# Gated cross-attention with an int8-style FFN on one core: attention rebuilt as a software pipeline, with operand turns by DMA and one block for both phases

## What is computed

```python
x = x + tanh(g_xattn) * xattn(layernorm(x), ctx)        # causal, softmax over 256 keys
x = x + tanh(g_ffn) * ffn(layernorm(x))
# xattn: q = xn @ Wq.T; k, v = split(ctx @ Wkv.T); softmax(causal(q k^T / sqrt(32))) v @ Wout.T
# ffn:   xq, w1q, w2q, hq are the operands rounded to 127 steps of their rows' maxima
#        gate, up = split(xq @ w1q.T); h = silu(gate) * up; hq @ w2q.T
```

## Time and profile before

| | us |
|---|---|
| median of 3 runs | 884.68 (880.06 to 885.18) |
| the profiled execution, its own time | 884.49 |
| its span in the profile | 882.4 |
| TensorE busy | 782.7 (89%) |
| VectorE busy | 638.7 (72%) |
| GpSimd busy | 518.5 (59%) |
| ScalarE busy | 418.2 (47%) |
| granted TensorE clock, mean | 0.955 of full |
| DMA | 135.98 MB |

### The profile page before, as it was taken

How to read it: one execution, slowest core, us unless ns; L and a number is a source line. 1 busy time by engine, 2 the same in 40 slices (tenths; PEclk the granted TensorE clock), 3 DMA queues, 4 the chain that set the end, 5 groups by cost and what they waited for, 6 DMA issues and landing times. The chain is left out here.

```text
span 882.4 us, 19003 instructions
## 1 busy us (share of the span) xinstructions
PE 782.7 (89%) x6146; PEld 564.8 (64%) x6168; DVE 638.7 (72%) x1997; ACT 418.2 (47%) x664; POOL 518.5 (59%) x671
## 2 busy tenths in 40 slices
PE   2579899998999989989999999897699999999994
PEld 2468787886877877868878778675444444444441
DVE  3575776876866867768678576476389999999992
ACT  5336456466375464563664645414234444444441
POOL 3525466474564663754745637324167888888885
PEclk9788899999999999999999999977899999999998
DMA  5784765775857757768668575406115655565666
GB/s 211 176 195 130 173 164 150 179 191 140 212 150 180 173 161 164 179 147 204 168 164 190 144 179 124 125 2 269 61 23 117 160 151 140 139 139 139 144 140 168
DMA packets 121889, 135.98 MB, mean 154 GB/s; under 512 B 73536, under 2 KB 84288, under 8 KB 121536
## 3 DMA queue, kind: packets, MB, share of 16 engines
q1 hardware_dynamic: 120768, 134.26, 60.0%
q10 hardware_dynamic: 1024, 0.53, 0.2%
HBM read 47.06 MB, written 25.30 MB: 82 GB/s over the span
## 5 line engine op out<-in xcount | busy, mean ns | idle before, releaser
L654 DVE CUSTOM_DVE_ANT_0 junk<-psum,mask 128x128 f32<-128x128 f32 (+1 forms) x512 | 159.4, 354 | 5.0 <-PE psum L843 3.2
L1172 PE MATMUL psum<-w1q,xqb 128*128 128x512 bf16 (+1 forms) x757 | 157.7, 363 | 3.3 <-PEq L255 1.9
L1072 POOL TENSOR_TENSOR up<-gate,up 128x512 f32<-128x512 f32 (+1 forms) x96 | 112.4, 1185 | 46.1 <-ACT gate L1098 38.3
L390 POOL TENSOR_SCALAR_AFFINE_SELECT prob<-prob 128x512 f32<-128x512 f32 x128 | 80.2, 638 | 94.5 <-ACT prob L588 87.0
L1172 PEld LDWEIGHTS psum<-w1q,xqb 128*128 128x128 bf16 x768 | 75.4, 98 | 83.9 <-issue 4.0
L1103 ACT ACTIVATE up<-up,round_bias,hinv 128x1408 f32<-128x1408 f32 x32 | 50.0, 1561 | 128.7 <-DVE hinv L1144 128.7
L588 ACT ACTIVATE prob<-psum 128x768 f32<-128x768 f32 x128 | 101.5, 827 | 18.4 <-PE psum L912 18.0
L910 PE MATMUL psum<-qs,ks 98*128 98x256 f32 x256 | 78.8, 369 | 23.8 <-DMA qs<-nmT 18.6
L1186 PE MATMUL psum<-w2q,hqT 128*128 128x512 bf16 x341 | 81.8, 389 | 7.4 <-DMA hqT<-hq 6.8
L910 PEld LDWEIGHTS psum<-qs,ks 98*128 98x128 f32 x256 | 50.8, 199 | 44.6 <-DMA qs<-nmT 25.9
L843 PE MATMUL psum<-ks,qs 96*128 96x256 f32 x256 | 76.1, 344 | 0.0
(11 more groups left out here) (126 smaller groups left out, 1904.2 us busy)
## 6 DMA issues: line engine op xcount, KB each, us to landing
ks<-k_hi SPq DMA_DIRECT2D x128, 128.0 KB, 2.7
qs<-q_hi SPq DMA_DIRECT2D x128, 128.0 KB, 2.4
xln<-x_dram SPq DMA_DIRECT2D x16, 512.0 KB, 5.0
ks<-k_lo SPq DMA_DIRECT2D x64, 128.0 KB, 2.5
qs<-q_lo SPq DMA_DIRECT2D x64, 128.0 KB, 2.9
x<-x_dram SPq DMA_DIRECT2D x16, 512.0 KB, 3.9
x_scratch<-x SPq DMA_DIRECT2D x16, 512.0 KB, 5.1
x1b<-x_scratch SPq DMA_DIRECT2D x32, 256.0 KB, 3.5
```

What stands on the lines that cost most here:

```text
L390: pool.affine_select(out=blk, in_=blk, compare_op=ALU.is_ge, fill=0.0, base=0, pattern=[[0, 4], [1, P]], channel_multiplier=-1).then_inc(s ...
L654: dve.tensor_tensor_reduce(junk[:, n % 2, 0:w], psum[:, h % 4, cols], m, 1.0, LOWEST, ALU.add, ALU.max, mx[:, par, t, h:h + 1]).then_inc(s ...
L1072: pool.tensor_tensor(up[:, t % 3, o], gate[:, t % 3, o], up[:, t % 3, o], ALU.mult).then_inc(f["prod_done"], 1)
L1172: last = pe.matmul(psum[:, n, 0:w], xqb[:, t % 4, k, :], w1q[:, k, half * I + o:half * I + o + w], start=(k == 0), stop=(k == KH - 1))
```

## The change

- All runs in one block. Slots b go from -2 to 16; tile 0 of the FFN stands between slots 15 and 16 on every engine, tiles 1 to 35 behind slot 16.
- In slot b, PE does the output of T = b-1, pass two and `weigh` of A = b, pass one of N = b+1, and transposes, keys, queries, values of F = b+2. Passes one and two alternate, two heads and one pair at a time. Pass one has banks 0 and 1, one head each, pass two has banks 2 and 3 for every pair. Reciprocals and both broadcasts of A lie at the end of the same slot.
- `WORK`, and with it the banks 6 and 7, is new.
- Weights are stored as rows and read back in slot 14 with two transposing DMAs; rounded x is stored as rows and loaded tile by tile with a transposing DMA. The scales go to DRAM in slot 13 and come back as broadcast loads. PE's and DVE's work on these is gone.
- `stand_alone`, which only incremented an unused semaphore, is gone. The FFN's operations are the same.

The diff, cut to its core:

```diff
-        WORK = [("K", 0, 1), ("K", 1, 1), ("Q", 0, 1), ("BC", 0, -1), ("BC", 1, -1), ("Q", 1, 1), ("V", 0, 1),
-                ("XT", 0, -2), ("O", 0, -1), ("O", 1, -1), ("V", 1, 1), ("XT", 1, -2), ("T", 0, 2), ("T", 1, 2),
-                ("W", 0, 1), ("W", 1, 1)]
+        WORK = [("O", 0, -1), ("O", 1, -1), ("T", 0, 2), ("T", 1, 2), ("K", 0, 2), ("K", 1, 2), ("Q", 0, 2),
+                ("BC", 0, 0), ("Q", 1, 2), ("BC", 1, 0), ("V", 0, 2), ("V", 1, 2)]
+        def run(eng, slot, tile):
+            for b in range(-2, B):
+                slot(b)
+            tile(0)
+            slot(B)
+            for t in range(1, NT + 4):
+                tile(t)
...
@@ sync
+                def load_x(tile):
+                    sp.wait_ge(s["xq_stored"], DMA * (tile // ST + 1))
+                    sp.dma_start_transpose(xqb[:, tile % 4], xq_scratch[tile]).then_inc(f[f"x_loaded{tile % 4}"], DMA)
+                def slot(b):
+                    A, F, T = b, b + 2, b - 1
+                    if b == B - 2:
+                        sp.wait_ge(s["q_moved"], DMA * MOVES * B)
+                        sp.wait_ge(s["k_moved"], DMA * MOVES * B)
+                        sp.wait_ge(s["v_done"], 2 * B)
+                        sp.wait_ge(s["w_stored"], DMA * PIECES)
+                        sp.wait_ge(s["steps_stored"], DMA)
...
+                        sp.dma_start_transpose(w1q[:], w1_scratch).then_inc(f["w1_loaded"], DMA)
+                        sp.dma_start(s1[:], rows[:, 0:2 * I].broadcast_to((P, 2 * I))).then_inc(f["steps_loaded"], DMA)
+                        sp.dma_start(s2[:], rows[:, 2 * I:NW * P].broadcast_to((P, H))).then_inc(f["steps_loaded"], DMA)
+                        sp.dma_start_transpose(w2q[:], w2_scratch).then_inc(f["w2_loaded"], DMA)
...
+                    if present(F + 1):
+                        sp.wait_ge(s["t_done"], 2 * (F + 1))
+                        sp.dma_start(xln[:], x_tok[F + 1]).then_inc(s["x_loaded"], DMA)
...
+                    if b == PIECES - 2:
+                        sp.wait_ge(s["gate_step"], 1)
+                        sp.dma_start(step_scratch.rearrange("n p -> p n"), w_scale[:],
+                                     allow_slow_non_contiguous=True).then_inc(s["steps_stored"], DMA)
+                    if present(T):
+                        sp.wait_ge(s["x1_done"], 2 * T + 2)
+                        sp.dma_start(x1_bat[T], x1[:]).then_inc(s["x1_stored"], DMA)
+                    if present(F):
+                        wait_for(sp, s["st_done"], PAIRS * (A + 1))
+                        spread_heads(k_hi, k_lo, ks, (0, 1, 0), s["k_moved"], s["k_hi"], s["k_lo"], F)
+                    if present(A):
+                        wait_for(sp, s["xn2_done"], 2 * (T + 1))
+                        wait_for(sp, s["x1_stored"], DMA * (T + 1))
+                        sp.dma_start(x1[:], x_tok[A]).then_inc(s["xres_loaded"], DMA)
+                    if present(F):
+                        spread_heads(q_hi, q_lo, qs, (0, 0, 1), s["q_moved"], s["q_hi"], s["q_lo"], F)
+                    if present(T):
+                        sp.wait_ge(s["xq_done"], 2 * T + 2)
+                        sp.dma_start(xq_bat[T], xq[:]).then_inc(s["xq_stored"], DMA)
...
@@ gpsimd, the order of one slot (low_o, select: batch A; quantise, rsqrt2: T; the others: F)
+                    split_context(); rsqrt1(); weights()
+                    if b == -2: tables()
+                    select(0); select(1); low_t(0); select(2); select(3); low_t(1); select(4)
+                    rsqrt2(); select(5); low_k(0); select(6); select(7); low_k(1)
+                    low_o(0); quantise(0); low_o(1); quantise(1)
@@ scalar, the order of one slot
+                    if b > -2: weights()
+                    exps(0); norm1(0); exps(1); norm1(1); exps(2); high_t(0); exps(3); copy_u(0)
+                    exps(4); high_t(1); exps(5); norm2(0); copy_u(1)
+                    if b == -2: high_weights("wq", wq_hi, wq_raw); weights()
+                    exps(6); high_k(0); exps(7); norm2(1); copy_u(2); high_k(1); copy_u(3)
+                    high_q(0); maxima_rows(); high_o(0); high_q(1); high_o(1); copy_v(0); copy_v(1)
@@ vector, the order of one slot
+                    measure_x()
+                    residual(0); measure(0); maxima(0); maxima(1); residual(1); maxima(2); maxima(3)
+                    measure(1)
+                    for h in range(4, NHEAD):
+                        maxima(h)
+                    negate(); reciprocals(); split_q(0); step(0); normalise(0); split_q(1)
+                    normalise(1); step(1); weigh_rows(b + 3)
+                    if b == PIECES - 2:
+                        dve.tensor_scalar(w_scale[:, W1T:NW], w_scale[:, W1T:NW], gates[:, 1:2], None,
+                                          ALU.mult).then_inc(s["gate_step"], 1)
@@ tensor
+                    def scores(h): ...
+                            wait_for(pe, s["max_done"], 2 * (NHEAD * N + h - 1))
+                    def score_pair(pair): ...
+                        wait_for(pe, s["exp_done"], PAIRS * A + pair)
+                    output(0, 0); output(0, 1); score_pair(0); output(1, 0); score_pair(1); output(1, 1)
+                    scores(0); scores(1); score_pair(2); transposed(0); scores(2); scores(3)
+                    score_pair(3); weigh(0); scores(4); scores(5); score_pair(4); transposed(1)
+                    scores(6); scores(7); score_pair(5); weigh(1); scores(8); scores(9)
+                    score_pair(6); keys(0); scores(10); scores(11); score_pair(7); weigh(2)
+                    scores(12); scores(13); keys(1); queries(0); scores(14); scores(15); weigh(3)
+                    queries(1); maxima_rows(); queries(2); broadcast(0); queries(3); broadcast(1)
+                    values(0); values(1)
```

More of the change, by code:

```diff
@@ L337, in _ @@
+                run(sp, slot, tile)
+                for p in range(2):
+                    sp.wait_ge(f[f"stored{p}"], DMA * NT // 2)
             @block.gpsimd
@@ L1106, in slot, with low_weights @@
                     silu(2)
[L1108 removed]
+                run(act, slot, tile)
             @block.vector
             def _(dve):
[L1112 to L1114 removed]
+                dve.memset(round_bias[:], ROUND).then_inc(s["table"], 1)
+                def low_weights(n, hi, lo, raw):
+                    dve.wait_ge(s["high"], n + 1)
+                    dve.tensor_tensor(lo[:], raw, hi[:].bitcast(F32), ALU.subtract).then_inc(s["split"], 1)
```

1373 lines of the change are left out of this document (624 added, 749 removed).

## The result

The change made the kernel slower: 959.05 us (median of 4, 947.73 to 960.87) against 884.93 us for the kernel before (4 runs, 880.06 to 886.74). The ratio is 1.0824, with a 95% interval of 1.0743 to 1.0904. The forecast was 916 us with a range of 880 to 945: the direction was right, the size was not, and the result lies outside the range. The profiled execution after took 960.04 us for a span of 958.3.

What follows compares the result with a forecast made beforehand. Attention was taken as bound by the in-order chain through TensorE with short waits, the FFN by TensorE. 109 + 12 x 37.6 + 50 + 52 + 252.3 gave a 914.3 span, plus 2.1: 916 us, range 880 to 945.

Steps and rivals of the forecast that it cites:

- The walk: Steady attention slot, followed operation by operation: 29 us of TensorE work plus 7.6 of waits, 36.6 in all.
- the 1.0 that the sum has for the clock: Steady slot: allowance for the granted clock falling behind two gaps of 2.2 us, taking a slot from 36.6 to 37.6.
- the 3.0 of its upper bound: Steady slot: most that clock falls were allowed to add, the upper bound of a slot being 39.6 us against 36.6.
- The rival in which the clock stays at 2.4 GHz: Steady slots: no clock fall, 12 slots of 36.6, time 904 us; chance 0.18.
- that of two falls in every slot: Steady slots: clock falls twice a slot, uncovered, 12 slots of 39.6, time 940 us; chance 0.08.
- The rival that ends faster: Steady slots: the norm2 wait is covered, a slot takes 34 or less, time 866 us; chance 0.13.
- with 2.5 for issue and drain of the steps: Slot 13: store of the weight scales taken at 2.5 us from a span of 2.5 to 16, slot about 50.
- a chance of 0.11 together with slow transposes: Rival: steps' store at 16 us, or transposes out of DRAM at half rate (+22), time 930 to 938; chance 0.11.
- The queue on SP: Slot 14: weight transposes, steps' broadcast and x take 28 us ahead of the x1 store; first FFN matmul at +52.
- the 45 without the queue: Drain, slot 14's first scores to the first FFN matmul: 45 us if SP's queue did not delay the x1 load.
- the queue hides: Drain rival: transposes run at the plain DMA rate, so SP's queue costs nothing, time 909 us; chance 0.08.
- 16 heads at 0.62: Start, behind the first scores: VectorE's maxima for 16 heads take 9.9 us, part of reaching batch 1's scores at 74.

Runs made afterwards that it cites:

- the first experiment: The changed kernel with slot 13's store of the weight scales issued behind the last batch's k and q moves instead of ahead: 941.87 us, ratio 1.067.
- third, the bank change: The changed kernel with the second half of the queries in bank 7 instead of 6 and values(0) ahead of broadcast(1): 952.66 us, ratio 1.0766.
- fourth: The changed kernel with norm2(0) on ScalarE behind exps(6) and high_k(0) instead of behind exps(5): 918.33 us, ratio 1.0383.
- fifth experiment: The changed kernel with useless matmuls put into TensorE's three waits in slots 1 to 13: 955.54 us, ratio 1.0808.
- the last kernels: The changed kernel with TensorE-turned scales, norm2(0) later, x1 load before weight transposes, low_t first: 885.81 us; also second queries in bank 7, high_q(1) before high_o(0): 875.87.

## Why the prediction was right or wrong

**Right: the steady slot.** The walk gave 36.6 at full clock, and the slots at full clock average 36.9. No row or run shows the 1.0 that the sum has for the clock, or the 3.0 of its upper bound; in their place the slots show 1.15 (the mean of 38.06 less 36.9) and at most 3.3 (40.2). Each wait that was named is there with its releaser, and the period, which was called the most dangerous term, missed by 0.46, or 5.5 us over 12 slots (0.9 a slot in the first experiment's trace of the same slots). The rival in which the clock stays at 2.4 GHz is refuted by the 1.2 GHz stretches in the trace, and so is that of two falls in every slot: five of the twelve slots have no such stretch, and only one (40.2) is beyond its 39.6.

**Right: the place of the cheap remedy.** The rival that ends faster named the `norm2(0)` wait and a slot of 34 or less. Its mechanism is real: with `norm2(0)` behind `exps(6)` the shortest slots take 34.0 and the mean is 35.3. The price was higher than the 2.25 us of the wait, for the clock goes with it.

**Wrong: slot 13, +18.4.** The step that failed is "with 2.5 for issue and drain of the steps". It is the largest miss: without it the span would have been 939.9. The wait for `gate_step` and the order on SP were right (51.8 measured with long pieces against 50), but of the two ends named, 2.5 and 16 us, the lower one was taken without a reason, and the store took 17.1 to land. The upper end came from a row that was misread. The 128 KB that landed in 4.8 us are 512 pieces of 256 bytes, not 1024; by the piece that makes 31 us for 3328, where 1024 would make 15.6. The trace has 5.1 ns a piece, so neither the bytes nor that row's pieces gave the size, and 16 was near by luck. The store also slowed its neighbours (804 ns a packet against 109) and left a backlog in which the last q move took 10.2 us to land, which no bound contained. The prediction gave this a chance of 0.11 together with slow transposes, and priced the two as one. The Trainium skill (DMA: Bandwidth & Descriptors, Rules for kernel authors) warns of turning data by a plain DMA with a rearranged access pattern and names a factor of 19 against a DMA transpose. The trace agrees with the warning (17.1 us for 13 KB), no run here shows the factor; the prediction did not draw on that rule, and it would have spoken for the upper end.

**Wrong: the drain, +6.6, for another reason than thought.** The queue on SP was forecast as 28 us ahead of the x1 store, with a cost of 7; it was 26.3 us (643.69 to 669.94), and then the wait for `exps` was 1.40. The rest is clock. The kernel with the useless matmuls has the same program in slots 14 and 15, a hole of 28.51 us and the load of x as late (+28.6 us against +29.6), and yet its drain is 52.9. The two windows do the same work at a granted clock of 0.69 in the kernel after and 0.82 in the other:

```profile
643.72:702.30 58.58, 47.38 (x378) 33.94 (x380) 24.43 (x96) 19.39 (x30) 16.44 (x28) 0.69 0.63 149
```

```profile
644.25:697.11 52.86, 40.27 (x379) 29.20 (x379) 24.23 (x96) 19.14 (x30) 16.48 (x28) 0.82 0.72 165
```

The half clock lasted 25.6 us behind the end of the hole in the kernel after, and 5.8, 12.5 and 6.5 us in the kernels of the third, fourth and fifth experiment, whose holes are 28.5 to 29.5 us and whose drains are 51.0, 51.8 and 52.9. So the hole does not settle it; what does, no run shows, and one profile of each kernel is all there is. Apart from the clock, the 45 without the queue was too low (48.4 and 48.5 in two kernels with the load of x ahead of the transposes) and the 7 for the queue too high (49.0 to 52.9 with it). That 52 was near these is two errors that cancel, and that is luck. The queue costs 10.44 only in the first experiment, where it is shorter (24.9 us) but starts 15.9 us behind `scores(0)`, since it waits for the steps.

On the transposes, the trace puts w1q (2816 KB) 13.4 us from issue to landing, against 11.2 for the plain load of the same size in the earlier trace rows; the forecast was 15 of transfer, with a latency of 1.7 taken off that has no row. Nor did the `hqT` row speak against the plain rate: its 360 KB land in 3.6 us, between these two plain rows of the old trace.

```profile
x<-x_dram SPq DMA_DIRECT2D x16, 512.0 KB, 3.9
...
x1b<-x_scratch SPq DMA_DIRECT2D x32, 256.0 KB, 3.5
```

The Trainium skill (Advanced Engine Details and Errata, X-Bar Transpose (TRN2)) says that they run as fast as ordinary DMAs, and this trace bears that out to within 20%; in the traces of the experiments the same transpose took up to 15.05, 34% more. But the rival built on it ("the queue hides") did not come about, since the transposes hold the issuing queue for 11.32 and 11.12 us, nearly their whole length, where the plain issues of this kernel take 0.4 to 0.6 us. What stands behind a transposing DMA on SP waits for it whatever the transfer's rate. The old trace had this already: one `hqT` transpose of 360 KB holds SP for 1.37 us, which by the size makes 11.0 for w1q.

```profile
701.51 1.37 SPq L1052 DMA_TRANSPOSE hqT<-hq  x1
```

**Wrong: the start, +7.6.** Here 16 heads at 0.62 were put down (9.9 us) as if VectorE's maxima set the pace, plus 3.1 for what follows up to `queries(2)`. That is 13.0, and the trace has 19.1 (49.38 to 68.47). Between the scores stand the transposes, keys and a quarter of the queries. With the scores themselves they are 7.4 us of TensorE at full clock by the prediction's own prices and twice that at 1.2 GHz, and 1.2 GHz is what it had up to 65.1: the window of the start has a mean clock of 0.71. The wait of 6.92 us for the moves in front of it is in the same trace. This reading rests on the trace alone, no run tried it. Another 1.9 us were lost before the first scores. GpSimd's order probably accounts for these and more: in the last kernels, where `low_t` goes first beside the other edits, the first scores start at 43.9 instead of 49.4.

**Small: FFN and tail, +3.7.** The output of the last batch between tiles 0 and 1 was counted as 5.6; the stretch is 9.3 longer than in the earlier trace rows. TensorE now waits 2.48 and 1.24 for VectorE's gate at 719.91 and 731.20. That VectorE has the last batch's work beside it there is the likely reason, which no run tried.

**The range.** Its upper end held slow pieces or two clock falls, not both in full, but no case in which the stage behind a hole runs at the lower clock for long. The two largest misses, 18.4 and 7.6, have nothing to do with each other; the range would have needed a case with the store at its upper bound as the likeliest one, about 930, and then some 15 us for the clock at the start and behind the hole.

## What to carry to other kernels

Count the pieces of a DMA, not its bytes: a 13 KB store in 4-byte pieces took 17 us, slowed what ran beside it (16.6 us together), and with the wait that stood in front of it in the same queue cost 29 us, where with one TensorE transpose in its place slot and drain showed no cost of it. In an in-order pipeline whose slot is closed by a loop (here q split, moves, scores), look at the whole loop before taking a wait away: `norm2(0)` held its start and no later step made up for it, while the bank change brought its start forward by 1.2 us and the moves gave all of it back. And a wait can cost more than its length when the clock falls behind it: 1.95 us of waiting were worth 2.74 us a slot.

## What the runs showed of the hardware

- A DMA transpose of 2816 KB held the queue of the engine that issued it for 10.5 to 12.3 us, a plain DMA for 0.4 to 0.6 us in most issues (3.42 in one behind the store in small pieces). The landing was 13.4 to 15.1 us after the start of the issue.
- Stores in 4-byte pieces: 3328 pieces took 17.1 us to land, the same bytes in 128 pieces 3.45 us. With 256 such pieces in nearly every slot the 16 KB maxima moves landed after 4.2 us instead of 2.7.
- Idle waits of 1.3 to 2.4 us in each slot were enough for the granted clock to fall to 1.2 GHz behind some of them (30.7 to 44.4 us over 12 slots). Filled with work, the falls went back to 10.2 us, with a kernel that was no faster.
- Behind the hole of 29.67 us TensorE was busy 24.9 of 25.2 us and still had 0.50 of its clock throughout; it was also at 0.50 while it idled (618 to 643). Behind holes of 28.5 to 29.5 us in three other kernels it was at full clock after 5.8 to 12.5 us.
